# One-core transformer block on Trainium2: in the graph units, the contexts go directly behind the score round and the round's second piece of maxima behind them

## The reference

```python
nodes = {-1: inputs}
for c in range(NUM_NOD):                                  # 6
    nsrc = min(c + 1, MAX_PREV)
    q = ew[c, 0] * (nodes[c - 1] @ We[eq] + be[eq])
    k = ew[c, 1] * (nodes[snode] @ We[ek] + be[ek])
    v = ew[c, 2] * (nodes[snode + nsrc // 2] @ We[ev] + be[ev])
    o = _mha(q, k, v, Wq[c], Wk[c], Wv[c], Wo[c])         # 8 heads of 16, softmax over 1024 keys
    nodes[c] = act_w[c] * o + q
out = nodes[NUM_NOD - 1]
return _layernorm(out, ln_g, ln_b)
```

## Time and profile before

| | |
|---|---|
| median of 3 runs | 3166.3 us (3165.73 to 3174.5) |
| the profiled execution | 3165.4 us, span 3163.4 us |
| mean granted clock of TensorE | 0.974 |
| TensorE busy | 2896.4 us, 92% of the span |
| VectorE busy | 2419.2 us, 76% |
| ScalarE busy | 2144.4 us, 68% |

### The profile page before, as it was taken

The page is one execution under the profiler, slowest core; times in us unless marked ns, Lnnn a source line. Parts: engine busy times, 40 slices in busy tenths (PEclk is TensorE's granted clock), DMA queues, the critical chain, the costliest instruction groups (busy, mean ns, idle before and its releaser), DMA issues. The chain is left out here.

```text
span 3163.4 us, 49154 instructions
## 1 busy us (share of the span) xinstructions
PE 2896.4 (92%) x19007; PEld 1293.5 (41%) x19007; DVE 2419.2 (76%) x3075; ACT 2144.4 (68%) x2683; POOL 380.2 (12%) x322
## 2 busy tenths in 40 slices
PE   5699999999779999999999999999999999999994
PEld 4356656665433333333333333333333333333331
DVE  6655656565868888888888888888888888888843
ACT  1155656555447777777777777777777777777783
POOL 0000000000001111111101111111111110111114
PEclk9699999999979999999999999999999999999996
DMA  6000000004244434435444444443453544345202
GB/s 178 18 11 2 28 2 22 8 23 82 59 94 77 104 93 88 111 93 111 75 100 95 94 104 99 86 97 94 88 110 97 107 74 105 95 88 110 53 22 88
DMA packets 144399, 243.90 MB, mean 77 GB/s; under 512 B 56562, under 2 KB 92934, under 8 KB 140838
## 3 DMA queue, kind: packets, MB, share of 16 engines
q1 hardware_dynamic: 143590, 238.67, 34.0%
q10 hardware_dynamic: 576, 2.10, 0.2%
HBM read 163.82 MB, written 74.10 MB: 75 GB/s over the span
## 5 line engine op out<-in xcount | busy, mean ns | idle before, releaser
L1598 ACT ACTIVATE pt_b<-ps_max 128x1024 f32<-128x1024 f32 x1516 | 1491.7, 1025 | 364.5 <-PE ps_max L1469 360.5
L1623 DVE TENSOR_REDUCE mx_b<-ps_pair 128x2 f32<-128x1024 f32 (+1 forms) x989 | 1193.5, 1207 | 166.9 <-PE ps_pair L1455 158.7
L1504 PE MATMUL ps_ctx<-pt_b,vs 128*32 128x512 f32 x6144 | 820.6, 606 | 3.8 <-ACT c_b L1587 3.5
L1623 DVE TENSOR_REDUCE mx_b<-ps_misc 128x1 f32<-128x512 f32 x989 | 677.7, 685 | 144.0 <-PE ps_misc L1455 125.7
L1469 PE MATMUL ps_max<-qs,ks 50*128 50x512 f32 x3032 | 780.4, 436 | 1.3 <-ACT part L1555 0.9
L1455 PE MATMUL ps_pair<-ks,qs 48*128 48x512 f32 x1955 | 512.3, 458 | 84.8 <-DVE mx_b L1623 84.6
L1469 PEld LDWEIGHTS ps_max<-qs,ks 50*128 50x128 f32 x3032 | 353.2, 186 | 344.0 <-ACT pt_b L1598 254.0
L1455 PE MATMUL ps_misc<-ks,qs 48*128 48x512 f32 x989 | 441.8, 447 | 7.1 <-DVE mx_b L1623 0.3
L960 ACT ACTIVATE pt<-ps_max,cb 128x512 f32<-128x512 f32 x340 | 215.0, 686 | 223.3 <-PE ps_max L801 159.5
L1455 PEld LDWEIGHTS ps_pair<-ks,qs 48*128 48x128 f32 x1955 | 207.4, 184 | 364.8 <-DVE mx_b L1623 332.5
L1455 PEld LDWEIGHTS ps_misc<-ks,qs 48*128 48x128 f32 x989 | 183.2, 185 | 333.4 <-DVE mx_b L1623 260.7
(11 more groups left out here) (194 smaller groups left out, 2257.6 us busy)
## 6 DMA issues: line engine op xcount, KB each, us to landing
partd<-part SPq DMA_DIRECT2D x22, 2048.0 KB, 9.1
qs<-partd SPq DMA_DIRECT2D x288, 128.0 KB, 5.6
ks<-partd SPq DMA_DIRECT2D x288, 128.0 KB, 6.7
xv<-node SPq DMA_DIRECT2D x26, 512.0 KB, 5.5
xf<-node SPq DMA_DIRECT2D x24, 512.0 KB, 4.7
node<-nt_b SPq DMA_DIRECT2D x48, 256.0 KB, 2.1
rec_b<-invd SPq DMA_DIRECT2D x368, 32.0 KB, 1.8
xq<-node SPq DMA_DIRECT2D x22, 512.0 KB, 3.8
```

Source lines behind the costliest of these rows:

```text
L1504: ins = pe.matmul(psO[SLOT * i:SLOT * i + SLOT, :], vs[u % 2][:, kb, QUAD * (s // HALF_STEPS) + i], pt[:, (QUAD * S + i) % ENTRIES], start ...
L1598: act.activation(pt[:, e:e + 2].rearrange("p k n -> p (k n)"), at[:], ACT.Exp, scale=SCALE_B).then_inc(exp_done, 1)
L1623: nc.vector.tensor_reduce(mx2[:, at:at + n], (psP, psX)[p % 2][:, 0:CHUNK * n].rearrange("p (h n) -> p h n", h=n), AX.X, ALU.max).then_inc ...
```

## The change

In `unit(u)` of TensorE, the loop over `steps_at(u, r)` moves ahead of the loop over `pieces_at(u, r, 1)`. Nothing else changes.

```diff
@@ -1530,10 +1530,10 @@
                             project(w, k, to[:, 0:CHUNK])
                         else:
                             output(w, k, to[:, 0:CHUNK])
+                        for S in steps_at(u, r):
+                            contexts(S)
                         for m in pieces_at(u, r, 1):
                             maxima(*m)
-                        for S in steps_at(u, r):
-                            contexts(S)
 
                 for u in range(UNITS):
                     unit(u)
```

## The result

The change makes the kernel slower: 3240.6 us (median of 4, 3239.4 to 3244.1) against 3166.0 us (median of 4), ratio 1.0232, 95% interval 1.0212 to 1.0252. The forecast was 3194, with a range up to 3224. The direction was right; the forecast size, 28 us, was less than half of the 74 us that came.

The account below looks back on a forecast made before the run. The prediction took each unit as bound by a loop between TensorE and VectorE, neither full. Its terms summed to +1.26 us a unit, x 23 = +29 us on 3165.4, giving 3194 us; range 3140 to 3224.

Parts of the forecast that it names:

- rounds 21 to 23: A free pair starts behind contexts, its reduce is late and the pair of round 23 waits: taken as +0.96 us.
- rounds 6 to 9: A blocked single lets contexts and the next score come earlier; the output round lets VectorE catch up: taken as -0.47 us.
- rounds 55 to 59: A blocked pair, then a free one: 0.82 us gained at round 56 is lost again at round 59's pair, +0.16.
- the list: Gains and losses worked for each changed round of a unit, some 0.1 us error a term, summing to +1.26 us.
- 31 and 33: Rounds following a late start that is absorbed there: -0.26 us a unit.
- Round 44: The changed round 44 was put at 0 us a unit.
- Distance 2: Time from a score round to contexts behind it: 0.33 us, or 0.56 if a single piece runs beside the round.
- the losses stay and nothing is won back: Upper bound: losses of 2.2 us and one more free single of 0.35, 2.55 us a unit, 59 us, 3224.
- Faster: Rival: VectorE's lag is absorbed while TensorE runs contexts at blocked pieces for nothing; 3144 us, chance 0.22.
- No change: Rival: gains and losses cancel within 0.4 us a unit; 3166 us, chance 0.15.
- A late piece is never won back: Rival: absorptions at rounds 6, 18 and 31 fail; 2.55 us a unit, 3224 us; 2 us or more given 0.15.
- The gain of the singles beside a score round: Eight singles moved beside the next score would save about 0.23 us each, 42 us; counted as nothing, paid a round later.

Follow-up runs that it names:

- e3: The kernel before with contexts moved ahead of the piece in round 21 alone, units 0 to 21: 3187.0 us, ratio 1.0066.
- e10: The kernel before with contexts moved ahead of the piece in rounds 57 and 69 alone (two ready pairs), units 0 to 21: 3210.3 us, ratio 1.0146.
- e2: The kernel before with the change only in the 10 rounds whose piece was ready, units 0 to 21: 3290.2 us, ratio 1.0393.
- e4: The kernel before with the opposite change in 13 other rounds, the next round's piece going ahead of contexts, units 0 to 21: 3246.2 us, ratio 1.0257.
- e8: The kernel before with the change in rounds 6 and 36 and the opposite in rounds 4, 42 and 48, units 0 to 21: 3175.8 us, ratio 1.0035.
- e1: The kernel before with the change only in the 9 rounds whose piece waited for VectorE, units 0 to 21: 3178.0 us, ratio 1.0040.
- e5: The kernel before, order unchanged, with VectorE's reduces reading half the columns and exponentials scaled by another 1/64: 3064.4 us, ratio 0.9686.
- e6: The changed order with VectorE's reduces reading half the columns and exponentials scaled by another 1/64: 3117.5 us, ratio 0.9851 to the kernel before.
- e7: The kernel before with contexts moved ahead of the piece in rounds 6 and 36 alone, units 0 to 21: 3152.6 us, ratio 0.9966.
- e9: The whole change except in rounds 1 and 73, units 0 to 21: 3230.7 us, ratio 1.0218 to the kernel before.
- e11: The whole change except in rounds 21, 38, 57 and 69, units 0 to 21: 3231.0 us, ratio 1.0206 to the kernel before.

## Why the prediction was wrong

**What was right.** The unit as a loop between TensorE and VectorE; VectorE's idle time grows by 81 us in the launch; the contexts' own waits cost next to nothing (5.5 us of idle time ahead of them in the launch, 3.8 before); the wait moves from rounds 26, 36, 55 and 67 to the pieces behind, to rounds 23, 28, 59 and 71 as said, and to 40, 46, 53 and 65 too, which were not named. The three worked places came close: rounds 21 to 23 +1.08 in the profile after (taken +0.96), rounds 6 to 9 -0.35 (taken -0.47), rounds 55 to 59 +0.18 (taken +0.16). The price of a ready pair is confirmed by e3 (+1.1 for one) and e10 (+2.2 for two).

**The step that failed** is the list, "worked so, round by round through the whole unit", with its "error of a term is some 0.1 us". The sum was +1.26 and is +2.75 (medians of the periods of units 1 to 21, 95.84 - 93.09). Term by term, from the shifts in the profile after:

| rounds | taken | measured |
|---|---|---|
| 73 and 1 | +0.1 | -0.12 |
| 6 | -0.47 | -0.35 |
| 12 | 0 | +0.13 |
| 18 | -0.2 | 0 |
| 21 | +0.96 | +1.08 |
| 26 | +0.36 | +0.32 |
| 31, 33 | -0.26 | +0.18 |
| 36, 38 | +0.1 | +0.19 |
| 44 | 0 | +0.40 |
| 51 | +0.35 | +0.38 |
| 55, 57 | +0.16 | +0.18 |
| 61, 63 | 0 | +0.18 |
| 67, 69 | +0.16 | +0.19 |

Ten of the thirteen terms are within 0.2; but nearly all the misses have one sign, and four of them (31 and 33, 44, 18, 61 and 63) make 1.2 of the 1.5 us. These are the places whose delay the list let be absorbed or put at nothing. All the others together make 0.3. Round 44 shows one cause. TensorE there, in the kernel after:

```profile
1722.18 0.52 PE L1469 MATMUL ps_max<-qs,ks 50*128 50x512 f32 x2
1722.76 1.06 PE L1504 MATMUL ps_ctx<-pt_b,vs 128*32 128x512 f32 x8
1723.76 0.50 PE L1455 MATMUL ps_misc<-ks,qs 48*128 48x512 f32 x1
...
1725.04 0.50 PE L1455 MATMUL ps_misc<-ks,qs 48*128 48x512 f32 x1 [0.32 <-DVE mx_b L1623]
1725.04 0.73 PE L1469 MATMUL ps_max<-qs,ks 50*128 50x512 f32 x2
1725.70 1.07 PE L1504 MATMUL ps_ctx<-pt_b,vs 128*32 128x512 f32 x8
1726.69 0.50 PE L1455 MATMUL ps_pair<-ks,qs 48*128 48x512 f32 x2
```

From the score to the contexts it is 0.58 us, where the 0.41 of the worked round 55 is shorter by 0.17, and in round 46 it is 0.66, where it was 0.56 before. Both lie on the path, since the next single waits for this one's reduce, and together they make 0.27 of the 0.40; the rest is open. Distance 2 was read at two places (0.33 and 0.56) and used at nineteen; over them it is 0.50 on average and up to 0.66. And where I let a stretch absorb (rounds 18, 31 and 33), nothing was absorbed: in e2, where no blocked place is changed, round 18 gives 0 and rounds 31 and 33 +0.18 too, and e3 shows that a late pair in round 21 keeps its +1.07 to the unit's end.

**What was not in the sum** is the clock. The profile before has a granted clock of 1.00 in every one of units 1 to 22, and I took that for granted. After, 16 of the 74 us are falls of the clock; without them the time would be at the upper edge of the range, 3224. They are bound to one place, 4.9 to 5.8 us into a unit in every kernel looked at (e2, e4 and e8 have them too, of 3.4 or 6.8 us), which is in round 3 or 4, behind the turn round with its thin TensorE work. Why some units have one and others, with the same timeline, don't, these runs don't settle. What the profiles show, one of each kernel, is that they vary with the order: none among units 1 to 21 in the kernel before, e1, e3, e5, e6, e7 and e10, two in e4 and e9, four in e2, e8 and after, thirteen in e11. That the order is the cause of each is not shown.

**The range** was closed above at 2.55 us a unit, "the losses stay and nothing is won back". That bound was built from my own list's terms, so it shared their error: e2 shows the losses to be 5.6 us a unit when nothing is won back. A bound should have come from the rows: ten ready places at one step of contexts, 10 us a unit.

**The rivals.** "Faster" fell in the way that its own condition said: round 59's pair had no slack. "No change" is out by 74 us. "A late piece is never won back" was nearest: its 3224 is 17 short of the time, and its reason is what e3 and e10 show. That its 59 us are just what the units lose without the clock (57 + 4 - 2) is in part luck: round 6 still wins 0.35 us, which it had given up, and round 44 loses 0.40, which it hadn't. The gain of the singles beside a score round, which I had not counted, didn't come: in the profile after, a single and round 7's score start together at 1672.66, and the next round then stands 0.90 us behind the score instead of 0.67. The 0.23 us that the partner saves are paid one round later, as the prediction had it.

## What to carry to other kernels

When two engines hand a double-buffered tile back and forth, put independent work on the first engine directly *behind* the instruction that feeds the second, so that it runs under the second's work; in front of a ready feed it costs its full length (0.97 of 1.00 us here), and a feed that isn't ready costs its wait to whatever stands behind it (0.7 to 1.0 us). In front of a feed that isn't ready the work costs little and gains as little (e1, +0.4% for nine places). Decide by place, with the time at which each instruction would come to stand, and change few: two of nineteen places gave 0.3%, all of them cost 2.3%. An advance that one engine gains is worth nothing by itself if its next instruction waits for the other engine.

## What the runs showed of the hardware that was not expected

**VectorE and GpSimd in one moment.** In e7, units lose up to 1.1 us at round 40, the place of the second of two small combinations in a unit. The small combination of the maxima (32 columns, SBUF to SBUF) takes 0.21 us in one unit and 1.26 in another. VectorE, slow case and then fast case:

```profile
1963.38 1.26 DVE L1636 TENSOR_TENSOR mx_b<-mx_b 128x32 f32<-128x32 f32 x1
1964.53 0.68 DVE L1628 TENSOR_REDUCE mx_b<-ps_misc 128x1 f32<-128x512 f32 x1
```

```profile
2056.78 0.21 DVE L1636 TENSOR_TENSOR mx_b<-mx_b 128x32 f32<-128x32 f32 x1
2056.89 0.68 DVE L1628 TENSOR_REDUCE mx_b<-ps_misc 128x1 f32<-128x512 f32 x1
```

GpSimd, at the slow one and at the fast one:

```profile
1963.28 1.28 POOL L1710 TENSOR_TENSOR cn_b<-c_b,rec_b 128x512 f32<-128x512 f32 x1 [18.48 <-DMA rec_b<-invd]
```

```profile
2056.83 1.29 POOL L1710 TENSOR_TENSOR cn_b<-c_b,rec_b 128x512 f32<-128x512 f32 x1 [18.59 <-DMA rec_b<-invd]
```

In the slow case GpSimd began 0.10 us before VectorE, and VectorE's instruction ended 0.08 us behind GpSimd's. In the fast case VectorE was first by 0.05 us and nothing happened to it. The reduces, which read PSUM, keep their time beside GpSimd (singles 687 ns when GpSimd is at work at their start and 685 when it isn't, in the kernel before). The other profiles say the same of all 598 such combinations in the thirteen kernels. The 174 that began while GpSimd was idle took at most 0.22 us, also the 30 in which GpSimd began meanwhile. Of the 424 that began while it was at work, 344 took over 0.30 us, up to 1.35, and each of these ended 0.07 or 0.08 us behind GpSimd's instruction. So such a combination lasts until GpSimd is done. An edit that moves GpSimd's instruction was not tried.

This is also the scatter of the units where round 36 is changed and rounds 21 and 38 aren't. In e1, e7, e8 and e11 a unit without a fall of the clock is longer by 0.9 to 1.0 us for each microsecond of its second combination (correlation 0.94 to 0.98). In e2 and e10 the same delay costs nothing, and the units agree within 0.1 us.

**The lower clock.** In the unit from 2145.9 us of the kernel after, the same groups show both levels; the first row is at the upper one, the second at the lower one.

```profile
2146.99 1.06 PE L1504 MATMUL ps_ctx<-pt_b,vs 128*32 128x512 f32 x8
...
2154.61 1.93 PE L1504 MATMUL ps_ctx<-pt_b,vs 128*32 128x512 f32 x8
```

From 2151.6 to 2161.8 us the granted clock is at half, which is 1.2 instead of 2.4 GHz. Contexts that give way to the next group after 1.00 us need 1.86 (2154.61 to 2156.47), and the unit takes 4.6 us longer than its neighbours.
